# Recurrent layers: Pool makes B products in pairs of 1024 columns in the ring of four; feed-forward weights in five wide pieces

## The reference

```python
def fp4_quant_dequant(x):                       # blocks of 16 along the last dimension
    xb = x.reshape(shape[:-1] + (shape[-1] // BLOCK, BLOCK))
    scale = jnp.maximum(jnp.max(jnp.abs(xb), axis=-1, keepdims=True) / 6.0, 1e-12)
    idx = jnp.searchsorted(_MID, jnp.abs(xb / scale))
    return (_GRID[idx] * jnp.sign(xn) * scale).reshape(shape)

def fp4_linear(x, w):
    return jnp.einsum('bsk,nk->bsn', fp4_quant_dequant(x), fp4_quant_dequant(w))

h = silu(fp4_linear(x, w_gate)) * fp4_linear(x, w_up)   # w_gate, w_up: 704 x 256
y = fp4_linear(h, w_down)                               # w_down: 256 x 704

def step(h, inp):                               # one token of a recurrent layer; h: 512 x 16
    dt_t, B_t, C_t, u_t = inp
    dA = jnp.exp(dt_t[:, :, None] * A)
    h = dA * h + (dt_t * u_t)[:, :, None] * B_t[:, None, :]
    return (h, jnp.einsum('bdn,bn->bd', h, C_t))
```

## Time and profile before

| what | value |
|---|---|
| median of three runs | 9607.7 us (9601.9 to 9612.53) |
| the profiled execution: its own time | 9595.9 us |
| its span, first to last instruction | 9594.1 us |
| mean granted TensorE clock | 0.942 |
| first recurrent layer, first scan to last item's end | 4632 to 6745 us |
| second recurrent layer | 6850 to 8870 us |
| `f0`: first weight instruction to first gate product | 3839.5 to 3921.7 us |

### The profile page before, as it was taken

One profiled execution on the slowest core, in us unless ns is written; L12 is line 12 of the kernel. 1 busy time (PEld: TensorE's weight loads), 2 busy tenths in 40 slices (PEclk: granted clock), 3 DMA queues, 4 the chain that ended last, 5 costly groups with the idle time before them and its releaser, 6 DMA issues. The chain is left out here.

```text
span 9594.1 us, 174060 instructions
## 1 busy us (share of the span) xinstructions
PE 8265.4 (86%) x48396; PEld 4733.9 (49%) x48396; DVE 8404.7 (88%) x13140; ACT 5621.0 (59%) x9217; POOL 5059.4 (53%) x4749
## 2 busy tenths in 40 slices
PE   5699999999999996698788888888688888888599
PEld 2366676667667665465333333333233333333366
DVE  5788888888888886898699999999599999999799
ACT  2377777777777772233566666665466665655233
POOL 1100000000000000586699999999599999999487
PEclk8799999999999998899899999999899999999799
DMA  7988888888888886111221112221221222221111
GB/s 233 302 281 283 282 281 282 281 283 281 282 282 281 281 282 189 50 43 44 85 81 68 59 76 81 81 81 43 93 75 70 80 90 90 90 88 54 48 43 40
DMA packets 1174167, 1447.39 MB, mean 151 GB/s; under 512 B 83658, under 2 KB 1053914, under 8 KB 1140992
## 3 DMA queue, kind: packets, MB, share of 16 engines
q1 hardware_dynamic: 1173824, 1444.18, 46.0%
HBM read 880.81 MB, written 564.60 MB: 151 GB/s over the span
## 5 line engine op out<-in xcount | busy, mean ns | idle before, releaser
L1970 POOL TENSOR_TENSOR mb_bx<-mb_dtu,mb_bc 128x512 f32<-128x512 f32 x2048 | 2664.9, 1326 | 13.2 <-DVE mb_hs L2070 7.2
L2213 PE MATMUL mb_y_ps<-mb_g,ident 128*128 128x512 f32 x4096 | 2194.3, 642 | 467.1 <-DVE mb_g L2030 235.8
L2257 ACT ACTIVATE mb_dA<-mb_dt,mb_a_neg 128x512 f32<-128x512 f32 x2048 | 1400.5, 688 | 1625.4 <-DVE mb_hs L2070 1088.7
L1406 POOL MEMSET f_magic<- 128x1 f32 x2 | 0.2, 99 | 3564.2 <-POOLq L127 3564.2
L2213 PEld LDWEIGHTS mb_y_ps<-mb_g,ident 128*128 128x128 f32 x4096 | 762.6, 198 | 1651.4 <-issue 720.4
L1017 ACT ACTIVATE at_tab<-at_e_ps 128x384 f32<-128x384 f32 x2064 | 1013.9, 491 | 780.7 <-PE at_e_ps L934 779.4
L1071 DVE TENSOR_REDUCE at_nmax<-at_s_ps 128x1 f32<-128x1024 f32 x1025 | 1255.4, 1225 | 35.2
L950 PE MATMUL at_pT_ps<-ident,at_probs 128*128 128x128 f32 x8192 | 1117.4, 279 | 102.8 <-ACT at_probs L1022 82.8
L1022 ACT ACTIVATE at_probs<-at_s_ps,at_nmax 128x1024 f32<-128x1024 f32 x1025 | 1141.7, 1114 | 61.4 <-DVE at_nmax L1071 39.6
L950 PEld LDWEIGHTS at_pT_ps<-ident,at_probs 128*128 128x128 f32 x8192 | 893.9, 141 | 412.3 <-ACT at_probs L1022 383.8
L2030 DVE TENSOR_TENSOR mb_g<-mb_hs,mb_bc 128x512 f32<-128x512 f32 x1472 | 993.8, 675 | 33.7 <-PE mb_y_ps L2213 32.5
(11 more groups left out here) (237 smaller groups left out, 14224.2 us busy)
## 6 DMA issues: line engine op xcount, KB each, us to landing
at_tables<-at_tab SPq DMA_DIRECT2D x1032, 384.0 KB, 3.9
at_skew<-at_tables SPq DMA_DIRECT2D x1030, 256.0 KB, 3.1
mb_bc<-mb_bc_rows SPq DMA_DIRECT2D x256, 1024.0 KB, 6.5
at_skew<-at_tables SPq DMA_DIRECT2D x773, 128.0 KB, 3.5
at_opnd<-at_q_st SPq DMA_DIRECT2D x130, 210.0 KB, 4.5
at_opnd<-at_kl_st SPq DMA_DIRECT2D x130, 210.0 KB, 4.7
at_opnd<-at_kr_st SPq DMA_DIRECT2D x130, 210.0 KB, 4.7
at_q_st<-st_parts SPq DMA_DIRECT2D x96, 256.0 KB, 4.3
```

The source lines that it names most:

```text
L1970: pool.tensor_tensor(bx[:, s % RINGS, :], dtu[:, c, :], bc[:, 0, n, :], ALU.mult).then_inc(s_bx, 1)
L2213: nc.tensor.matmul(y_ps[:, c % 2, :], ident[:, :], g[:, s1 % RINGS, :], start=False, stop=(n == STATE - 1)).then_inc(s_y, 1)
L2257: nc.scalar.activation(dA[:, s % DA_RING, :], dt[:, c, :], ACT.Exp, scale=a_neg[:, c, n:n + 1]).then_inc(s_dA, 1)
```

## The change

In the recurrent layers Pool makes the products of slots `s` and `s + 1` (`s` even) in one instruction of 1024 columns, with `dtu[c]` read twice. The ring keeps its four places. A pair therefore waits until the scan of slot `s - 3` is done (before, slot `s` waited for the scan of slot `s - 4`), and the scans of both slots wait for the whole pair. `RINGS` becomes `BX_RING` and `G_RING`, both 4; nothing changes for `g`.

In the feed-forward parts the block `turn_weights` goes. The weights are loaded in five pieces: the two halves of `w_down` (704 columns each), the first 640 rows of `w_gate` and of `w_up` (five row blocks side by side, 1280 columns each), and their last 64 rows together (256 columns). Their preparation becomes a function `prepare(k)` on each engine that stands between the first bodies of the tile pipeline: 0, 1 and 2 before body -4, 3, 4 and 5 before bodies -3, -2 and -1. On DVE a piece now takes seven instructions; the multiplication that makes the rounding constant goes to ScalarE, the scale and the final scaling go to Pool. The load of `mod` is issued after those of the weights and of the first two tiles.

```diff
-        turn_weights(nc, f"{name}_w", ident, jobs)
...
+        widths = (FFN, FFN, edge // P * D, edge // P * D, D)
...
+        def run(eng, body, prepare):
+            for k in range(2):
+                prepare(k)
             for n in range(-4, 4):
+                if n + 6 <= jobs:
+                    prepare(n + 6)
                 body(Tile(n // 2, n % 2), *stages(n))
...
+            for k in range(2):                                        # SyncE
+                sp.dma_start(part(raw, k), w_down[k * P:(k + 1) * P, :]).then_inc(s_raw[k], 16)
...
+            def prepare(k):                                           # GpSimd
+                if k < jobs:
+                    pool.wait_ge(s_wfront, FRONT * k + 1)
+                    pool.tensor_scalar(part_blocks(wscale, k), part_blocks(wamax, k), 1.0 / 6.0, 1e-12,
+                                       ALU.mult, ALU.max).then_inc(s_wscale, 1)
+                if k > 0:
+                    pool.wait_ge(s_wscale, k)
+                    pool.wait_ge(s_wback, BACK * k)
+                    out = blocks_of(part(made, k - 1))
+                    pool.tensor_tensor(out, out, spread(wscale, k - 1), ALU.mult).then_inc(s_wq, 1)
+                if k == 3:
+                    pool.wait_ge(s_mod, 16)
...
+            def prepare(k):                                           # VectorE
+                if k < jobs:
+                    front = Steps(dve, s_wfront, FRONT * k)
+                    src, out = part(raw, k), part(made, k)
+                    dve.wait_ge(s_raw[k], 32 if k == 4 else 16)
+                    front(v.tensor_reduce(part_blocks(wamax, k), blocks_of(src), axis=AX.X, op=ALU.max, apply_absolute_value=True))
+                    front(v.tensor_scalar(part_blocks(wstride, k), part_blocks(wamax, k), TIGHT / 6.0, TIGHT * 1e-12,
+                                          ALU.mult, ALU.max))
+                    front(v.reciprocal(part_blocks(winv, k), part_blocks(wstride, k)))
+                    front(v.tensor_tensor(blocks_of(out), blocks_of(src), spread(winv, k), ALU.mult))
+                    front.issued(v.tensor_scalar(part(wtmp, k).bitcast(U32), out.bitcast(U32), STEP_BITS, None, ALU.bitwise_and))
+                if k > 0:
+                    back = Steps(dve, s_wback, BACK * (k - 1))
+                    out, tmp = part(made, k - 1), part(wtmp, k - 1)
+                    dve.wait_ge(s_wstep, k)
+                    back(v.tensor_tensor(out, out, tmp, ALU.add))
+                    back.issued(v.tensor_tensor(out, out, tmp, ALU.subtract))
...
+            def prepare(k):                                           # ScalarE
+                if k < jobs:
+                    act.wait_ge(s_wfront, FRONT * (k + 1))
+                    nc.scalar.activation(part(wtmp, k), part(wtmp, k), ACT.Identity, bias=magic[:, :],
+                                         scale=MAGIC_STEP).then_inc(s_wstep, 1)
...
+                act.wait_ge(s_wT, m + 1)
...
-                        ge(pool, s_scan, k.n * SLOTS + s - RINGS + 1)
-                        pool.tensor_tensor(bx[:, s % RINGS, :], dtu[:, c, :], bc[:, 0, n, :], ALU.mult).then_inc(s_bx, 1)
+                        if n % 2 == 0:
+                            r = s % BX_RING
+                            ge(pool, s_scan, k.n * SLOTS + s - BX_RING + 2)
+                            pool.tensor_tensor(bx[:, r:r + 2, :], dtu[:, c:c + 1, :].to_broadcast([P, 2, BANK]),
+                                               bc[:, 0, n:n + 2, :], ALU.mult).then_inc(s_bx, 2)
```

More of the change, by code:

```diff
@@ L1282, in ffn_phase, with part, blocks_of, part_blocks @@
         wd = sb("wd", [P, FC, D])
[L1283 to L1290, removed]
-        turn_weights(nc, f"{name}_w", ident, jobs)
+        edge = FFN // P * P
+        tail = FFN - edge
+        widths = (FFN, FFN, edge // P * D, edge // P * D, D)
+        starts = tuple(sum(widths[:k]) for k in range(len(widths)))
+        jobs = len(widths)
+        raw = sb("w_raw", [P, sum(widths)])
+        made = sb("w_made", [P, sum(widths)])
+        wtmp = sb("w_tmp", [P, sum(widths)])
+        wamax, wstride, winv, wscale = (sb(n, [P, sum(widths) // BLOCK]) for n in ("w_amax", "w_stride", "w_inv", "w_scale"))
+        def part(a, k):
+            return a[:, starts[k]:starts[k] + widths[k]]
+        def blocks_of(a):
+            return a.rearrange("p (n k) -> p n k", k=BLOCK)
+        def part_blocks(a, k):
+            return a[:, starts[k] // BLOCK:(starts[k] + widths[k]) // BLOCK]
+        def spread(a, k):
+            return part_blocks(a, k).unsqueeze(2).to_broadcast([P, widths[k] // BLOCK, BLOCK])
         mod = sb("mod", [P, batches, 3, D])
@@ L1382, in _ @@
             load_xr(Tile(0, 0))
+            for k, w in ((2, w_gate), (3, w_up)):
+                sp.dma_start(part(raw, k).rearrange("p (i d) -> p i d", d=D),
+                             w[0:edge, :].rearrange("(i p) d -> p i d", p=P)).then_inc(s_raw[k], 16)
+            for at, w in ((0, w_gate), (tail, w_up)):
+                sp.dma_start(part(raw, 4)[at:at + tail, :], w[edge:FFN, :]).then_inc(s_raw[4], 16)
+            sp.dma_start(mod[:, :, :, :].rearrange("p b k d -> p b (k d)"), mods.rearrange("b k d -> b (k d)")
+                         .unsqueeze(0).to_broadcast([P, batches, 3 * D])).then_inc(s_mod, 16)
             for t in range(2, 6):
@@ L1541, in body @@
                     hstep.issued(v.tensor_tensor(hd, hd, htmp[:, :], ALU.subtract))
-            run(dve, body)
+            run(dve, body, prepare)
         @block.tensor
         def _(pe):
+            def prepare(k):
+                if k == 0:
+                    return
+                m = k - 1
+                w = part(made, m)
+                pe.wait_ge(s_wq, m + 1)
+                ge(pe, s_wkept, m)
+                if m < 2:
+                    for c in range(FC):
+                        cw = min(P, FFN - c * P)
+                        mm = nc.tensor.transpose(turned_down[0:cw, c * P:(c + 1) * P], w[:, c * P:c * P + cw], ident[:, :])
+                elif m < 4:
+                    for i in range(edge // P):
+                        for c in range(DC):
+                            mm = nc.tensor.transpose(turned_up[:, c, i * P:(i + 1) * P],
+                                                     w[:, i * D + c * P:i * D + (c + 1) * P], ident[:, :])
+                else:
+                    for c in range(DC):
+                        mm = nc.tensor.transpose(turned_up[:, c, 0:P], w[:, c * P:(c + 1) * P], ident[:, :])
+                mm.then_inc(s_wT, 1)
+                if k == jobs:
+                    pe.wait_ge(s_wkept, jobs)
             def body(t, early, ahead, norm, turn, middle, hturn, last):
@@ L1587, in body @@
                         mm.then_inc(s_gate if at == 0 else s_gu, 1)
-            run(pe, body)
+            run(pe, body, prepare)
         @block.scalar
@@ L1632, in body @@
                                          gu_ps[:, 0:2, 0:HALF], ACT.Silu).then_inc(s_silu, 1)
-            run(act, body)
+            run(act, body, prepare)
 SLOTS = IC * STATE
@@ L1655 @@
 AT_LN, AT_HCENTER, AT_HSCALE = 53, (58, 59), 61
-RINGS = 4
+BX_RING, G_RING = 4, 4
 DA_RING = 2
```

45 lines of the change are left out of this document (31 added, 14 removed).

## The result

The changed kernel takes 9659.1 us (median of 5 runs, 9651.4 to 9665.5) against 9607.6 for the kernel before (9601.9 to 9612.5): ratio 1.0054, 95% interval 1.0044 to 1.0065. It is 51.5 us slower; 9623 was forecast, inside the range.

The account below looks back on a forecast made before the run. The prediction took DVE and Pool, both nearly full and handing work to each other in every slot, as the bound. Recurrent layers +81 and feed-forward weights -66 gave +15 on 9607.7, about 9623 us; 8-in-10 range 9545 to 9680.

Parts of the forecast that it names:

- Feed-forward, -66: Feed-forward weight stretch: 49.3 us to the first gate product for 82.2, saving 33 a phase, 66 in two.
- The pair, 2.34: Recurrent layers: one 1024-column Pool product takes 2.34 us, against 2.50 for two singles back to back.
- what Pool saves: Recurrent layers: a pair saves 0.16 us, 5 us an item, 164 us of Pool's time.
- the recurrent term: Recurrent layers get longer by 15 x 3.0 + 15 x 2.4 = 81 us.
- The steps that I worked out for slots 41 to 52: Delays per item: second layer +0.5 at scan 44, +1.05 line 2094, +1.25 line 2098; first layer +1.8 at slot 52.
- slots 0 to 40 come out within 0.1 of before: Walk through an item of the recurrent layers: pairs change slots 0 to 40 by at most 0.1 us.
- Waits of scans for `mb_bx` about the same sum: Expected sign: DVE's waits for Pool's product keep about their 100.6 us, now before even slots alone.
- `mb_v` with the same mean: Expected sign: DVE's `mb_v` in the recurrent layers keeps its mean duration, 1.76 us before.
- Pool's room absorbs the coarser hand-over: Rival: Pool runs further ahead, recurrent layers -30 to +45; 9542 us at 0 in the layers; chance 0.2, faster.
- Pool is the bound: Rival: Pool's saving counts, all 100.6 us of waits go, layers under -30; 9442 us; chance 0.1, faster.
- the fourth case: Rival: every DVE instruction that stands, stands longer, `mb_v` caught more often; layers over +115, 9672 us; chance 0.2, slower.
- The lower bound: Recurrent layers: at 1.93 us a pair, four pairs on the paths take 0.4 less each, giving +20.

Follow-up runs that it names:

- e3: As e2, but the scan of the even slot waits for both products, as for a pair; 9641.0 us, ratio 1.0043.
- e8: Changed kernel with a ring of eight (dt, dtu keep two chunks) and pairs issued two slots earlier in Pool's order; 9455.8 us, ratio 0.9851.
- e2: Changed kernel with each pair cut into two single products side by side at the even slot, same ring wait; 9512.3 us, ratio 0.9905.
- e9: Changed kernel with pairs issued two slots earlier in Pool's order, still in the ring of four; 9728.8 us, ratio 1.0138.
- e11: As e8, but with 512-column products issued two at a time in place of pairs; 9509.1 us, ratio 0.9909.
- e10: As e8, but with single 512-column products, each issued at slot p - 2, in place of pairs; 9498.7 us, ratio 0.9893.

## Why the prediction came out as it did

**Feed-forward, -66: right.** 70.3 saved; the first gate product came 46.97 us after the first weight instruction, 49.3 forecast.

**The pair, 2.34: right; what Pool saves: too small.** Median 2.353, mean 2.367. But the single products took 1.326 on the mean, since some stood behind DVE, so the products' time fell by 292 us and not 164. Pool's busy time in the layers fell by 222 us. None of it reached the span.

**Direction and mechanism: right, the size of the recurrent term too small,** +81 forecast, +122.8 measured. Split by slots, from the periods between scans:

| | slots 1 to 40 | 41 to 52 | 53 to 0 |
|---|---|---|---|
| forecast | 0 | 15 x 1.8 + 15 x 3.3 = 76 | 15 x 0.6 - 15 x 0.3 = 5 |
| first layer | +21.4 | +25.8 | +9.5 |
| second layer | +12.4 | +48.1 | +5.7 |

The steps that I worked out for slots 41 to 52 sum to 76 and measured 73.9. One by one, over 15 items: slot 44 with the shorter slot 41 +0.25 and +0.4 (+0.5 forecast), line 2199 2.73 long (2.7), line 2203 3.03 in the second layer and 1.2 in the first (3.0 and 1.1), scan 48 of the first layer +1.07 (+1.1), pair 52 +0.37 (+0.3).

**The step that failed** is "slots 0 to 40 come out within 0.1 of before": 33.8 us of the missing 42. Three things were not in it. At slot 26 I set 1.2 against 1.1 and it is 0.17 longer. At slot 30 the pair stands behind the norm's small instructions, and DVE's idle time goes from 0.13 to 0.54; I had taken that for regained. Slots 26 and 30 together are 19.4 us. And there is a path that the walk did not follow at all: DVE's own `mb_g`, which reuses a place of a ring of four, waits for PE's sum into `mb_y_ps`. Who waited for whom on tile `mb_g` after (32.5 us in 66 places before), and one such place:

```profile
  DVE mb_g L2135: 47.3, 89
```

```profile
5587.13 0.69 DVE L2135 TENSOR_TENSOR mb_g<-mb_hs,mb_bc 128x512 f32<-128x512 f32 x1 [1.31 <-PE mb_y_ps L2318]
```

That is slot 18 of six items of the first layer (+1.4 each) and, with 0.4, slot 38 of 19 items; the two slots are 17.9 us. At both PE is late because its granted clock has fallen, and not because Pool's `mb_g` is later (PE's waits for Pool's `mb_g` fell from 631.4 to 490.0 us). PE before that place, and at the same place of the next item, where DVE did not wait:

```profile
5582.48 2.94 PE L2272 MATMUL mb_ring<-mb_outT,mb_yz 128*128 128x256 f32 x8 [1.95 <-ACT mb_u L2415]
5585.22 2.67 PE L2318 MATMUL mb_y_ps<-mb_g,ident 128*128 128x512 f32 x4
...
5717.53 1.99 PE L2272 MATMUL mb_ring<-mb_outT,mb_yz 128*128 128x256 f32 x8 [1.82 <-ACT mb_u L2415]
5719.36 1.88 PE L2318 MATMUL mb_y_ps<-mb_g,ident 128*128 128x512 f32 x4
```

and the windows of these two stretches (us, busy time of each engine, clock, DMA):

```profile
5583.45:5587.13 3.68, 3.68 (x8) 2.19 (x7) 2.37 (x3) 2.14 (x5) 3.68 (x3) 0.55 0.00 0
5717.13:5720.84 3.71, 3.31 (x12) 2.20 (x12) 3.71 (x7) 2.03 (x4) 3.71 (x3) 1.00 0.00 0
```

In the first the granted clock is 0.55, for the most part the lower level of 1.2 GHz, and from then on a matmul into `mb_ring` takes 0.63 us; in the second it is 1.00 (2.4 GHz) and the matmul takes 0.38. PE had stood for `mb_u` just before in both, 1.95 and 1.82 us. Without the first and the last item of each layer, the six items of the first layer with the low clock at slot 16 are the six in which DVE waits. Slot 38 follows slot 30 in the same way: there, with the product late, PE stands 2.1 us for `mb_u` where it stood 1.5 before, in 19 of the 28 items the granted clock then falls to the lower level for 3.4 us, and in these 19 and no others DVE waits at slot 38. In the kernel before, the clock falls at slot 30 in none of the 28 and at slot 16 in one, and that one has the 1.3 us wait. A low clock is not enough by itself: in e3 it falls at slot 30 in 17 items and DVE does not wait at slot 38. No run holds the clock fixed, so that the late product brings the fall about is argued from the longer standing of PE and not shown.

The other part is the end of the item, +15.2 for +5: in the first layer `mb_src` at line 2227 meets a pair and is 2.81 long for 1.72, where I had put slots 61 and 62 as a gain; in the second `mb_v` at slot 58 grew by 0.2 to 0.3.

**"Waits of scans for `mb_bx` about the same sum": wrong,** 149.0 for 100.6. That they stand before even slots alone is right. The wait at slot 26, which I called the largest, was not: before, slot 0 has 30.6 us and slot 26 has 16.3. **"`mb_v` with the same mean": right,** its standing over 128 instructions went from 139.9 to 142.6 us; but inside it slot 40 fell from 2.41 to 1.80 and slot 58 rose from 1.75 to 2.38.

**The rivals.** That Pool's room absorbs the coarser hand-over is false in a ring of four and true in e8: the absorbing case needs the pair issued earlier and a place to put it. That Pool is the bound is false: Pool's busy time fell by 222 us in the layers and they got longer. By its number (over +115) the fourth case came true, and only in part by its mechanism: the 1024-column instructions of DVE stand 115.8 us for 62.5, but `mb_v` is not caught more often.

**Standing and waiting.** My steps held about 46 us of longer standing of DVE and 35 of longer waits (an estimate from the steps of the prediction). The traces have 47.3 and 75.6. So the standing was sized right, and the term that was too small is the waiting. That fits e3, where the late hand-over alone, with no wide instruction, costs +122.7. The lower bound was also added up wrongly: four pairs an item that are 0.4 shorter are 48 us over 30 items, so it should have been +33 and not +20.

**Who gets in.** The Trainium skill, page "SBUF — State Buffer", section "Who interferes with whom", has DVE's two-input instruction and Pool's exclude each other first come first served. The runs agree that they exclude each other for a whole instruction, and not on the order: `mb_v`, which takes 0.67 us when nothing holds it, stood through three Pool instructions in e2 (3.77 us), and through two in the earlier trace rows.

## What to carry to other kernels

Merging two small instructions of a producer saves its issue time and delays the first half of what it makes by almost one instruction. Look at every consumer that waits for the first half, and at everything behind the merged instruction in the producer's order (in e9 `mb_g`, then PE, then DVE), not only at the producer's busy time; if the producer is not the bound, the saving is worth nothing by itself. Look also at what stands idle because of the new waits: here PE stood 0.6 us longer at slot 30, in 19 items its clock fell, and in those DVE waited eight slots later. The cure was not to give the merge back but to give it lead: earlier in the order and room in the ring, both at once, since room alone gave 31 us, order alone lost 68, and the two together gave 203. Mending the merge only at the places where waits are seen moves the waits to the next place.

## What the runs showed of the hardware

When `mb_v` on DVE stands behind Pool, it does not always get in when the Pool instruction under way ends. With Pool's instructions back to back at slot 40, it took 2.41 on the mean (through the rest of one and all of a second) in the kernel before, 3.56 in e2 and 3.92 in e11 (the rest of one and all of two), but 0.83 in e3, where it started 0.2 to 0.4 before the end of a product, and 1.80 and 2.10 behind a pair in the changed kernel and e8, where it had stood 1.0 to 1.6. In e2, e10 and e11 it was the narrow instructions that kept DVE out longer: two of them and an `mb_g` make one stretch that it did not enter, and behind a pair it entered at the first end. In the slow cases it got in only when Pool itself had stopped: the next Pool instruction, `mb_dt`, stood 0.7 us for `mb_v` in 30 of 32 items in the kernel before and in e2, in 32 in e10 and 31 in e11, and in none in e3, e8 and the changed kernel. When it gets in otherwise is not settled: in the second layer of e3 it started 0.9 before the end at slot 58 and was passed over, in the first layer 1.1 before and was not. I know no rule that covers all of these.
